# A four-layer transformer on one core: jobs of two layers take turns, a shorter prologue, and three areas for attention weights

## The chip, the cores and the metric

The kernel runs on one core of one Trainium2 chip. The metric is the device time of one launch in microseconds (us). Each core has a matrix engine (TensorE, in the rows PE, with its weight loads as PEld), a vector engine (VectorE, DVE), a scalar engine (ScalarE, ACT), GpSimd (POOL), and SyncE (SP), which here only issues transfers. Each engine works through its own list of instructions in order; they wait for each other by semaphores.

## The reference

Sixteen sequences of 256 tokens by 256 channels go through four different transformer layers, in float32. H is 16 heads of 16 channels; the context has 77 tokens of 256 channels.

```
x: (16, 256, 256)   context: (16, 77, 256)   cond: (16, 256)
L0: x += gate * self_attention(modulated_norm(x), rope, mask)
    x += gate * cross_attention(modulated_norm(x), context, key mask)
    x += gate * mlp(modulated_norm(x))           # gelu(tanh)
L1: x += cross_attention(modulated_norm(x), modulated_norm(context))
L2: x += gate * self_attention(...) ; x += cross_attention(...) ; x += gate * mlp(...)
L3: x += self_attention(..., rope)  ; x += cross_attention(..., rope) ; x += mlp(...)
modulated_norm(x) = norm(x) * (1 + scale) + shift
scale, shift, gate = (cond or silu(cond)) @ W + b    # ten pairs and five gates in all
```

## The kernel before, in words

**Jobs.** One sequence in one layer is a job; there are 64, numbered 0 to 63. Jobs 0 to 15 are L0, 16 to 31 L1, 32 to 47 L2, 48 to 63 L3. The text calls them "the first layer" to "the fourth layer" or L0 to L3. A job needs the stored result of the same sequence in the layer before. A job holds one of six slots (SLOTS), its number modulo six, from its start to its end, so that at most six jobs are under way; x, xhat, xnT and other tiles exist once per slot.

**Steps.** Each job is a list of steps, each one belonging to one engine. Self attention: the norm (ln, rs, nx), its transpose (xT, xe), projections (qkv), the split of queries and keys into a high and a low part (hi, lo), a round trip of these through memory that lays them out as stacked rows of q_stack and k_self or k_cross (ph, pw, lh, ll), scores by rows (S, `score_rows`) with row maxima on VectorE (mr, mx), the maxima placed by a transfer (sd), scores by columns (ST, `score_columns`), exponentials (ex), the weighted sums (W), transposes and division (oX, dv, atT), the output projection (out) and the residual (res). Cross attention is the same with 77 keys; the mlp has four steps up and two down.

**The plan.** `Program` writes out the order of each engine by playing the steps through a table of costs: each engine takes, of the steps whose buffers are free, the one with the lowest 12 * job - rank, rank being the cost of the chain behind it inside its job. Buffers are rings: four banks gen and two banks score of PSUM, three of max_tok and maxT (MAXIMA), three transposed contexts (CTX_T), four q_stack, and so on.

**Weights.** The attention blocks have two areas of SBUF, A and B, the mlp one, M. L0 self is in A, L0 cross in B, L1 in A, L2 self in B, L2 cross in A, L3 self in B, L3 cross in A. `load_weights` is a step of SyncE: it waits for the last user of the area in all 16 jobs and then issues the loads, so L2's cross weights wait for the last job of L1, L3's self weights for L2's last self block and L3's cross weights for L2's last cross block.

**Prologue.** A block of its own ahead of the main program. SyncE issues the constants, then all modulation matrices (7.8 MB with the rest), six small biases b_qk and the constant rows of k_self and k_cross. TensorE forms all ten modulations (line 698, 80 products) and five gates (706 and 707), VectorE adds the biases (668 to 679), the gates are stored to memory (607), and the main block starts. Its first instructions load the weights of L0 (1008) and the first x (934).

```
st = min(can, key=lambda st: (12 * st.job - st.rank
         - 4 * (eng == "pe" and TILES.get(st.name, "whole") == self.tiles), 0))
...
done = max(st.after, key=lambda res: res.nth_all)
sp.wait_ge(*moved(done.fill))
for dst, src in weight_dmas(st.blk):
    sp.dma_start(dst, src).then_inc(w_loaded[st.blk.area], 16)
```

## Time and profile before

| what | us |
|---|---|
| median of three runs | 2927.14 |
| lowest and highest run | 2912.56 and 2935.08 |
| the profiled execution, its own time | 2929.03 |
| its span, first to last instruction | 2927.2 |
| TensorE busy in the span | 2747.2 (94%) |
| VectorE, ScalarE, GpSimd busy | 1986.1, 1431.8, 288.1 |
| mean granted clock of TensorE | 0.963 |

The profile is of one execution. A granted clock of 1.00 is 2.4 GHz. Start times in the rows are counted from the first instruction. Matmuls overlap one another, so a busy time near the whole of a stretch does not say that the engine is at its peak; the busy time of the weight loads (PEld) is a second measure of the work done in it.

### The profile page before, as it was taken

What the parts mean: (1) busy time and instruction counts of PE and PEld (TensorE: products, weight loads), DVE (VectorE), ACT (ScalarE), POOL (GpSimd) and SP (SyncE); (2) the same over time, 40 slices, a digit from 0 to 9 for tenths busy, and PEclk for the clock granted to TensorE, in tenths of its full rate; (3) what the DMA queues carried; (4) which work ended last, traced back from release to release, by engine and by line L of the source; (5) the groups of instructions that cost most, each with busy time, mean ns of one, the idle gap of its engine ahead of it and who ended that gap; (6) DMA issues with size and microseconds to landing.
All of it is one profiled execution on the core that took longest, in us unless ns stands there. A gap on an engine that the chain in (4) does not pass through costs nothing.

```text
span 2927.2 us, 57672 instructions
## 1 busy us (share of the span) xinstructions
PE 2747.2 (94%) x21122; PEld 2021.6 (69%) x21122; DVE 1986.1 (68%) x5340; ACT 1431.8 (49%) x2281; POOL 288.1 (10%) x340
## 2 busy tenths in 40 slices
PE   6789999999999999989999999999989999999998
PEld 5456776776766766666677777776656777777666
DVE  2676776776765577777576777766677778777751
ACT  0335455455454445445455555554545554555553
POOL 0000000100101111101111111111000000000000
PEclk9999999999999999988899999999989999999999
DMA  4544334334333466644444444424245343433320
GB/s 130 154 151 138 110 115 133 104 118 130 104 96 113 125 193 183 186 145 127 147 136 138 127 143 121 149 82 151 77 135 170 90 141 106 134 113 120 121 73 15
DMA packets 279966, 369.40 MB, mean 126 GB/s; under 512 B 32506, under 2 KB 159034, under 8 KB 279372
## 3 DMA queue, kind: packets, MB, share of 16 engines
q1 hardware_dynamic: 247436, 318.63, 36.4%
q10 hardware_dynamic: 32256, 47.07, 4.4%
q8 instruction: 177, 2.90, 0.4%
q14 instruction: 97, 0.79, 0.1%
HBM read 224.49 MB, written 110.97 MB: 115 GB/s over the span
## 4 chain that ended last, share of the span: by engine, by line
PE 68%; DVE 17%; DMA 5%; issue 5%; ACT 1%; SPq 1%; POOL 0%; ACTq 0%; DVEq 0%; POOLq 0%
PE gen L1219 11%; PE gen L1228 10%; PE gen L1094 9%; PE gen L1060 9%; PE gen L1177 8%; DVE row_max L1516 6%; PE score L1152 4%; PE score L1107 3%; PE score L1122 3%; DMA parts_scratch<-parts 2%; PE gen L1188 2%; PE score L1136 2%; PE score L1158 2%; PE gen L1069 2%; DVE maxT L1535 2%
## 5 line engine op out<-in xcount | busy, mean ns | idle before, releaser
L1516 DVE TENSOR_REDUCE row_max<-score 128x4 f32<-128x1024 f32 (+1 forms) x640 | 651.8, 1044 | 131.1 <-PE score L1136 99.5
L1338 ACT ACTIVATE probs<-score 128x1024 f32<-128x1024 f32 (+1 forms) x576 | 567.3, 1023 | 289.5 <-PE score L1152 174.6
L1219 PE MATMUL gen<-xnT,w_w1M 128*128 128x256 f32 x1536 | 380.8, 397 | 1.9 <-ACT xnT L1283 1.8
L1228 PE MATMUL gen<-w_w2M,hT 128*128 128x256 f32 x1536 | 353.9, 384 | 8.1 <-DVE x L1567 4.7
L1370 POOL TENSOR_TENSOR rstd<-var_eps,minus_half 128x2 f32<-128x2 f32 x160 | 113.1, 707 | 2270.3 <-DVE var_eps L1413 2256.1
L1219 PEld LDWEIGHTS gen<-xnT,w_w1M 128*128 128x128 f32 x1536 | 290.1, 196 | 55.8 <-issue 2.8
L1228 PEld LDWEIGHTS gen<-w_w2M,hT 128*128 128x128 f32 x1536 | 286.1, 191 | 57.8 <-issue 18.9
L1283 ACT ACTIVATE xnT<-gen,mod_all 128x256 f32<-128x256 f32 x288 | 147.0, 565 | 211.2 <-PE gen L1069 205.7
L1360 ACT ACTIVATE hT<-gen,b_b 128x256 f32<-128x256 f32 x384 | 160.2, 472 | 170.4 <-PE gen L1219 169.5
L1345 ACT COPY oT<-gen 128x512 f32<-128x512 f32 x224 | 131.7, 588 | 182.8 <-PE gen L1177 180.2
L1535 DVE STREAM_TRANSPOSE maxT<-max_tok 32x64 f32<-32x64 f32 x896 | 209.0, 233 | 17.1
L1122 PE MATMUL score<-k_self,q_stack 64*128 64x256 f32 x1536 | 194.0, 342 | 25.3 <-DVE row_max L1516 23.8
L1177 PE MATMUL gen<-probs,v_self 128*17 128x256 f32 x3072 | 203.7, 386 | 0.0
L1565 DVE TENSOR_TENSOR xhat<-gen,gate 128x256 f32<-128x256 f32 (+1 forms) x112 | 60.2, 538 | 204.9 <-PE gen L1228 141.1
L1122 PEld LDWEIGHTS score<-k_self,q_stack 64*128 64x128 f32 x1536 | 128.5, 191 | 100.2 <-issue 81.4
L1152 PE MATMUL score<-q_stack,k_self 64*128 64x256 f32 x1536 | 187.3, 341 | 10.7 <-DMA q_stack<-maxT 5.4
L1152 PEld LDWEIGHTS score<-q_stack,k_self 64*128 64x128 f32 x1536 | 126.7, 194 | 75.3 <-issue 51.1
L1136 PEld LDWEIGHTS score<-k_cross,q_stack 64*128 64x128 f32 x2048 | 139.7, 195 | 49.4 <-issue 47.0
L1136 PE MATMUL score<-k_cross,q_stack 64*128 64x78 f32 x2048 | 158.5, 288 | 9.2 <-issue 3.9
L1177 PE MATMUL gen<-probs,v_cross 77*17 77x256 f32 x2048 | 159.9, 402 | 6.3 <-DVE parts L1477 2.8
L1188 PE MATMUL gen<-ident,oT 128*128 128x128 f32 x896 | 145.6, 288 | 0.1
L1544 DVE RECIPROCAL row_max<-gen 128x16 f32<-128x16 f32 x224 | 54.9, 245 | 128.4 <-PE gen L1188 127.8
(146 smaller groups left out, 4172.9 us busy)
## 6 DMA issues: line engine op xcount, KB each, us to landing
q_stack<-parts_scratch SPq DMA_DIRECT2D x336, 256.0 KB, 3.8
parts_scratch<-parts ACTq DMA_DIRECT2D x160, 256.0 KB, 2.8
parts_scratch<-parts SPq DMA_DIRECT2D x160, 256.0 KB, 3.3
k_self<-parts_scratch SPq DMA_DIRECT2D x144, 256.0 KB, 3.9
q_stack<-zeros_scratch SPq DMA_DIRECT2D x112, 256.0 KB, 3.9
q_stack<-maxT SPq DMA_DIRECT2D x224, 128.0 KB, 2.7
k_cross<-parts_scratch SPq DMA_DIRECT2D x192, 78.0 KB, 2.5
x_scratch<-x SPq DMA_DIRECT2D x48, 256.0 KB, 2.6
```

The source lines that it names most:

```text
L1060: mm = pe.matmul(out, xT[:, fc], weight[:, fc, cols], start=fc == 0, stop=fc == FC - 1)
L1094: mm = pe.matmul(out[:, c, :], weight[:, fc, cols], xT[:, fc, :], start=fc == 0, stop=fc == FC - 1)
L1122: mm = pe.matmul(buf[:, t, c * S:c * S + S], queries[rows, column(u), c * P:c * P + P], keys[rows, column(u), :], start=not blk.mask, stop ...
L1136: mm = pe.matmul(buf[:, t, at_col:at_col + CTXP], queries[rows, column(2 * u + i), c * P:c * P + P], keys[rows, column(2 * u + i), :], sta ...
L1152: mm = pe.matmul(buf[:, t, kc * S:kc * S + S], keys[rows, column(u), kc * P:kc * P + P], queries[rows, column(u), :], start=not blk.mask, ...
L1177: mm = pe.matmul(pv[VW * i:VW * i + VC, within, :], value, e, start=kc == 0, stop=not blk.whole or kc == TC - 1, skip_group_check=True)
L1188: mm = pe.transpose(buf[:, at_col:at_col + P], oT[before.buf][:, i, c * P:c * P + P], ident[:, :])
L1219: mm = pe.matmul(buf[:, i * S:i * S + S], w["M"]["w1"][:, fc, col:col + P], xnT[s][:, fc, :], start=fc == 0, stop=fc == FC - 1)
L1228: mm = pe.matmul(buf[:, 0:D], hT[:, j, c * P:c * P + P], w["M"]["w2"][:, j, :], start=j == 0, stop=j == FFC - 1)
L1338: act.activation(probs[st.probs][0:keys, :, :], score[st.fill.buf][0:keys, :, :].rearrange("p a (r q) -> p (a r) q", r=2), ACT.Exp, bias=k ...
L1516: dve.tensor_reduce(dst, src, AX_X, ALU.max).then_inc(max_done[b], 1)
L1535: ins = dve.transpose(maxT[st.got["max"]][:, :, 32 * b:32 * b + 32].bitcast(F32), max_tok[st.got["max"]][32 * b:32 * b + 32, :, :].bitcast ...
```

## The change

**Turns.** A table JOBS gives each job its layer and sequence. After L0 and the first eight jobs of L1, jobs of L2 and L1 alternate: L2 sequence 0, L1 sequence 8, L2 sequence 1, L1 sequence 9, ... up to L2 sequence 7, L1 sequence 15; then L2 sequences 8 to 15, then L3. Numbers of jobs, and with them slots and priorities, follow the table.

**Areas.** A third area C takes L1 and L3 self: its q and out parts lie in the two mask tiles (maskk and maskq, used by L0 self only) and its kv part is a new tile. L2 self is now in A, L2 cross in B, L3 cross in A. L1's biases have tiles of their own. To make room, MAXIMA and CTX_T go from three to two.

**Prologue.** Only L0's three modulations and gates are formed ahead of the main block. The other seven modulations (steps md on TensorE, ma on VectorE) and two gates (mg, mh, and the store ms) are steps of the plan; their matrices are loaded into tiles that are not yet in use (w1, w2, kv of B, hT), five in the prologue and two (la) in the main program. L0's self weights and the first two x are loaded in the prologue. The weights of L0's cross and mlp wait for the sums that read those tiles. The small biases are issued by GpSimd.

```diff
-MAXIMA = 3
+MAXIMA = 2
-CTX_T = 3
+CTX_T = 2
...
-    [Block("L1", "cross", "A", 1e-5, mod=3, qk_bias=0, out_bias=True, ctx="norm", ctx_mod=4)],
-    [Block("L2", "self", "B", 1e-6, mod=5, qk_bias=2, out_bias=True, gate=3),
-     Block("L2", "cross", "A", 1e-6, qk_bias=4, out_bias=True, ctx="norm"),
+    [Block("L1", "cross", "C", 1e-5, mod=3, qk_bias=0, out_bias=True, ctx="norm", ctx_mod=4, behind=(0, 0))],
+    [Block("L2", "self", "A", 1e-6, mod=5, qk_bias=2, out_bias=True, gate=3),
+     Block("L2", "cross", "B", 1e-6, qk_bias=4, out_bias=True, ctx="norm"),
...
-    [Block("L3", "self", "B", 1e-5, mod=7, rope=S),
+    [Block("L3", "self", "C", 1e-5, mod=7, rope=S),
...
+GATES_EARLY = 3
+LATE = [Late("adaln2", 0, 3 * D, "w1", "M", 5, D, 0, True, gate=3),
+        Late("adaln2", 3 * D, 3 * D, "w2", "M", 6, D, 0, True, gate=4),
+        Late("adaln3a", 0, 2 * D, "kvB", "B", 7, 0, D, False),
+        Late("adaln1q", 0, 2 * D, "hT0", "hid", 3, 0, D, True),
+        Late("adaln1kv", 0, 2 * D, "hT1", "hid", 4, 0, D, True),
+        Late("adaln3b", 0, 2 * D, "hT0", "hid", 8, 0, D, False, then=3),
+        Late("adaln3c", 0, 2 * D, "hT1", "hid", 9, 0, D, False, then=4)]
+LEAD = 8
+JOBS = [(0, seq) for seq in range(B)] + [(1, seq) for seq in range(LEAD)]
+for turn in range(B - LEAD):
+    JOBS += [(2, turn), (1, LEAD + turn)]
+JOBS += [(2, seq) for seq in range(B - LEAD, B)] + [(3, seq) for seq in range(B)]
...
+        w["C"] = {"q": maskk[:, :, :].bitcast(F32), "kv": sb("w_kvC", shapes["kv"]), "out": maskq[:, :, :].bitcast(F32)}
...
-                    for dst, src in const_loads:
+                    for dst, src in const_loads[:4]:
                         sp.dma_start(dst, src).then_inc(const_loaded, 16)
-                    for key, name in ada_loads:
-                        sp.dma_start(ada[key][:, :, :], a[name].rearrange("(c p) n -> p c n", p=P)).then_inc(adaln_loaded[key], 16)
...
+                    sp.dma_start(ada[:, :, :], a["adaln0"].rearrange("(c p) n -> p c n", p=P)).then_inc(adaln_loaded, 16)
...
+                    for st in plan.order["sp"]:
+                        if st.early and st.name == "ldw":
+                            for dst, src in weight_dmas(st.blk):
+                                sp.dma_start(dst, src).then_inc(w_loaded[st.blk.area], 16)
...
+                    for i, late in enumerate(LATE):
+                        if late.then is None:
+                            dst, src = late_dma(i)
+                            sp.dma_start(dst, src).then_inc(late_loaded[i], 16)
...
+                def modulation_sums(st):
+
+                    late = LATE[st.j]
+                    pe.wait_ge(late_loaded[st.j], 16)
+                    buf, c = fill(st), siluT if late.silu else condT
+                    for kind, first in enumerate((late.scale, late.shift)):
+                        for fc in range(FC):
+                            col, n = first + fc * P, kind * FC + fc
+                            for kc in range(FC):
+                                mm = pe.matmul(buf[:, n * B:n * B + B], wide[late.tile][:, kc, col:col + P], c[:, kc, :], start=kc == 0, stop=kc == FC - 1)
+                    mm.then_inc(gen_full[st.buf], 1)
```

The diff changes the order of the instructions in three places of which the prediction speaks. TensorE's list at the start of the main program, before, from the second branch on: transposes of the first x (xhat), projections from area A, the context's from area B, then the first scores with their mask product.

```order
L1034 UNCONDITIONAL_BRANCH
L1069 MATMUL gen<-ident,xhat 128x128 x8
L1094 MATMUL gen<-xnT,w_qA 128x256 x8
L1094 MATMUL gen<-xnT,w_kvA 128x256 x8
L1060 MATMUL gen<-w_kvA,xnT 128x256 x8
L1080 MATMUL gen<-ident,ctx_in 128x77 x4
L1094 MATMUL gen<-ctxT,w_kvB 128x77 x8
L1060 MATMUL gen<-w_kvB,ctxT 77x256 x4
L1107 MATMUL score<-maskq,pick 128x512 x4
L1122 MATMUL score<-k_self,q_stack 128x256 x4
```

The same place now, in two pieces:

```order
L1124 UNCONDITIONAL_BRANCH
L1330 MATMUL gen<-condT,w_kvB 128x16 x8
L1159 MATMUL gen<-ident,xhat 128x128 x4
L1330 MATMUL gen<-siluT,w_w1M 128x16 x8
L1184 MATMUL gen<-xnT,w_qA 128x256 x4
```

```order
L1150 MATMUL gen<-w_kvB,ctxT 77x256 x2
L1330 MATMUL gen<-siluT,w_w2M 128x16 x8
L1197 MATMUL score<-maskq,pick 128x512 x4
L1212 MATMUL score<-k_self,q_stack 128x256 x4
L1197 MATMUL score<-maskq,pick 128x512 x4
L1212 MATMUL score<-k_self,q_stack 128x256 x4
L1330 MATMUL gen<-siluT,hT 128x16 x8
L1197 MATMUL score<-maskq,pick 128x512 x4
L1212 MATMUL score<-k_self,q_stack 128x256 x4
L1197 MATMUL score<-maskq,pick 128x512 x4
L1212 MATMUL score<-k_self,q_stack 128x256 x4
L1330 MATMUL gen<-siluT,hT 128x16 x8
```

Late sums (line 1330) now stand first, between the first transpose and its projection, ahead of the first scores, and between pairs of them; two late gates follow among the scores and two more sums among the first ST.

SyncE's list around the load of L2's cross weights (in_L_cq, in_L_ckv, in_L_co), before:

```order
L968 DMA q_stack<-zeros_scratch 32x4x512
L978 DMA q_stack<-parts_scratch 32x4x512 x2
L988 DMA q_stack<-parts_scratch 32x4x512
L1008 DMA w_qA<-in_L_cq 128x2x256
L1008 DMA w_kvA<-in_L_ckv 128x2x512
L1008 DMA w_outA<-in_L_co 128x2x256
L1008 DMA b_ckv<-in_L_bkv 128x256
L1008 DMA b_co<-in_L_bo 128x256
L968 DMA q_stack<-zeros_scratch 32x4x512
L1001 DMA x_scratch<-x 128x2x256
```

and now:

```order
L1056 DMA k_cross<-parts_scratch 32x4x156
L1036 DMA q_stack<-zeros_scratch 32x4x512
L1081 DMA w_qB<-in_L_cq 128x2x256
L1081 DMA w_kvB<-in_L_ckv 128x2x512
L1081 DMA w_outB<-in_L_co 128x2x256
L1081 DMA b_ckv<-in_L_bkv 128x256
L1081 DMA b_co<-in_L_bo 128x256
L1024 DMA parts_scratch<-parts 128x512
L1000 DMA x_in<-x_scratch 128x2x256
```

Before, the load stood beside the store of L1's last job, at place 655 of 1281 rows; now it stands at place 441, beside L1's third job, where L0's last cross block ends.

TensorE's list in the middle of L1, before, where all steps are L1's (weights in A):

```order
L1094 MATMUL gen<-ctxT,w_kvA 128x77 x4
L1060 MATMUL gen<-w_kvA,ctxT 77x256 x2
L1199 MATMUL gen<-ident,xhat 128x128 x4
L1136 MATMUL score<-k_cross,q_stack 128x78 x8
L1158 MATMUL score<-q_stack,k_cross 77x256 x4
L1069 MATMUL gen<-ident,xhat 128x128 x4
L1060 MATMUL gen<-w_outA,xnT 128x256 x4
L1158 MATMUL score<-q_stack,k_cross 77x256 x8
L1177 MATMUL gen<-probs,v_cross 17x256 x4
L1094 MATMUL gen<-xnT,w_qA 128x256 x4
```

and now, in the stretch of turns (self scores with k_self and w1 of L2, w_kvB from L2 cross, w_kvC, maskq and maskk from L1):

```order
L1150 MATMUL gen<-w_kvB,ctxT 77x256 x2
L1184 MATMUL gen<-ctxT,w_kvC 128x77 x4
L1150 MATMUL gen<-maskq,xnT 128x256 x4
L1212 MATMUL score<-k_self,q_stack 128x256 x8
L1159 MATMUL gen<-ident,xhat 128x128 x4
L1212 MATMUL score<-k_self,q_stack 128x256 x4
L1309 MATMUL gen<-xnT,w_w1M 128x256 x4
L1212 MATMUL score<-k_self,q_stack 128x256 x4
L1242 MATMUL score<-q_stack,k_self 128x256 x4
L1309 MATMUL gen<-xnT,w_w1M 128x256 x12
```

Steps of an L1 job stand between those of three L2 jobs at different stages.

## Rows read from the trace of the kernel before

**Rows 1.** The page, parts 1 and 2: busy times, and 40 slices of TensorE.

```profile
PE 2747.2 (94%) x21122; PEld 2021.6 (69%) x21122; DVE 1986.1 (68%) x5340; ACT 1431.8 (49%) x2281; POOL 288.1 (10%) x340
...
PEclk9999999999999999988899999999989999999999
```

**Rows 2.** Busy time by stretch; columns as in the first line.

```profile
core 0: us, PE busy (x) PEld busy (x) DVE busy (x) ACT busy (x) POOL busy (x), PEclk, DMA share, GB/s
75.00:250.00 175.00, 145.83 (x1232) 99.91 (x1234) 118.82 (x276) 65.30 (x99) 5.12 (x8) 0.93 0.47 147
300.00:850.00 550.00, 538.34 (x4442) 394.19 (x4439) 378.69 (x954) 273.93 (x420) 42.86 (x52) 1.00 0.38 117
1060.00:1204.00 144.00, 134.94 (x1136) 96.80 (x1132) 107.60 (x373) 73.17 (x133) 23.40 (x28) 0.91 0.61 183
1204.00:1460.00 256.00, 231.88 (x1774) 161.21 (x1774) 173.23 (x477) 119.01 (x192) 28.81 (x34) 0.88 0.49 148
1600.00:1875.00 275.00, 275.00 (x2149) 205.99 (x2149) 204.18 (x556) 151.36 (x246) 46.87 (x53) 1.00 0.44 133
1950.00:2250.00 300.00, 273.39 (x2000) 201.01 (x1999) 211.57 (x550) 151.05 (x236) 26.25 (x29) 0.93 0.41 128
2300.00:2750.00 450.00, 433.09 (x3353) 322.89 (x3351) 353.00 (x908) 242.48 (x382) 30.22 (x36) 0.99 0.39 121
```

**Rows 3.** Timeline, SyncE: loads of weights after L1 and L2, stores of finished jobs.

```profile
1060.93 0.38 SPq L1001 DMA_DIRECT2D x_scratch<-x  x1
...
1204.93 0.38 SPq L1001 DMA_DIRECT2D x_scratch<-x  x1
...
1374.32 0.39 SPq L1008 DMA_DIRECT2D w_qA<-in_L_cq  x1
...
1636.08 0.38 SPq L1001 DMA_DIRECT2D x_scratch<-x  x1
...
1873.02 0.38 SPq L1001 DMA_DIRECT2D x_scratch<-x  x1
...
1996.01 0.39 SPq L1008 DMA_DIRECT2D w_qB<-in_L_qkv  x1
...
2145.36 0.39 SPq L1008 DMA_DIRECT2D w_qA<-in_L_cq  x1
```

**Rows 4.** Timeline, the prologue and the first steps of the main program.

```profile
14.06 10.39 PE L698 MATMUL gen<-condT,ada 128*128 128x16 f32 x48 [3.90 <-DMA ada<-in_adaln]
...
44.77 3.57 PE L698 MATMUL gen<-condT,ada3c 128*128 128x16 f32 x16
...
48.27 1.89 PE L706 MATMUL score<-ada,condT 128*16 128x256 f32 x4
...
51.05 1.89 PE L706 MATMUL score<-ada,condT 128*16 128x256 f32 x4
...
61.21 1.03 PE L707 MATMUL score<-gate_bias,ones 1*16 1x256 f32 x2
...
65.26 0.40 SPq L1008 DMA_DIRECT2D w_qA<-in_L_qkv  x1
...
71.12 0.75 DVE L1407 BATCH_NORM_STATS2 stats<-x_in 128x6 f32<-128x256 f32 x2 [8.43 <-DMA x_in<-in_x]
...
75.20 1.09 PE L1069 MATMUL gen<-ident,xhat 128*128 128x128 f32 x4 [12.95 <-DVE xhat L1419]
```

**Rows 5.** Timeline of TensorE at the first scores.

```profile
105.40 1.03 PE L1107 MATMUL score<-maskq,pick 64*128 64x512 bf16 x4 [10.89 <-DMA k_self<-parts_scratch]
...
111.84 0.61 PE L1107 MATMUL score<-maskq,pick 64*128 64x512 bf16 x4 [0.29 <-DVE row_max L1516]
...
112.97 0.61 PE L1107 MATMUL score<-maskq,pick 64*128 64x512 bf16 x4 [0.29 <-DVE row_max L1516]
113.21 0.60 PE L1122 MATMUL score<-k_self,q_stack 64*128 64x256 f32 x4
115.45 0.61 PE L1107 MATMUL score<-maskq,pick 64*128 64x512 bf16 x4 [1.64 <-DVE row_max L1516]
```

**Rows 6.** The page, parts 5 and 6: ScalarE's move of xT; the maxima's transfer, us to landing.

```profile
L1283 ACT ACTIVATE xnT<-gen,mod_all 128x256 f32<-128x256 f32 x288 | 147.0, 565 | 211.2 <-PE gen L1069 205.7
...
q_stack<-maxT SPq DMA_DIRECT2D x224, 128.0 KB, 2.7
```

**Rows 7.** Stores of jobs (L1001): first and last start of the group.

```profile
L1001 SPq DMA_DIRECT2D x_scratch<-x x48: 360/377/594, 285.9 to 2205.8; - x48
```

**Rows 8.** Weight loads of one projection, in 1060 to 1204 and on the page.

```profile
L1060 PEld LDWEIGHTS gen<-w_outA,xnT 128*128 128x128 f32 x72 | 15.7, 227 | 2.7
...
L1228 PEld LDWEIGHTS gen<-w_w2M,hT 128*128 128x128 f32 x1536 | 286.1, 191 | 57.8 <-issue 18.9
```

More of the change, by code:

```diff
@@ L134, in __init__ @@
         self.buf = self.n = None
+        self.early = False
         self.prior, self.got, self.times = {}, {}, {}
@@ L204, in __init__ @@
         self.step, self.steps, self.ends, self.weights = {}, [], {}, {}
-        for job in range(len(LAYERS) * B):
+        self.gates_late = []
+        self.late_modulations()
+        for job in range(len(JOBS)):
             self.job_steps(job)
@@ L234, in job_steps @@
         kept = self.ends.get((job - SLOTS, "stx"))
-        last = early = self.add(job, 0, first, "ldx", 0, "sp", [self.ends.get((job - B, "stx"))])
+        last = early = self.add(job, 0, first, "ldx", 0, "sp", [self.ends.get((PLACE.get((li - 1, seq)), "stx"))])
+        if job < X_IN:
+            self.load_early(last)
         gate_free = left
@@ L1279, in modulated @@
                 def modulated(st, out, buf, pair, width, stride):
+                    if pair >= GATES_EARLY and not late_known:
+                        late_known.append(True)
+                        act.wait_ge(mod_added, len(LATE))
                     for fc in range(FC):
```

339 lines of the change are left out of this document (213 added, 126 removed).

## The prediction

> **What bounds the kernel now.** I read the busy times first. TensorE is busy 2747.2 of 2927.2 us, the next engine 1986.1, so TensorE's list sets the time, and its gaps, with the slices in which its granted clock is under 9 tenths or so, are where something can be won [rows 1]. Then the stretches. From 1600 to 1875 us, the steady part of L2, TensorE is busy in all of 275.0 us at a granted clock of 1.00, and its weight loads fill 205.99, a share of 0.749 [rows 2]. No change of order can win anything there. Four stretches are looser: the start (75 to 250, clock 0.93), L1 (1060 to 1204, clock 0.91), the passage into L2 (1204 to 1460, clock 0.88) and that into L3 (1950 to 2250, clock 0.93) [rows 2]. VectorE has 107.6 of 144 us in L1, ScalarE less, so neither is the bound there either; what is missing is TensorE's time, in short gaps and in slower matmuls.
>
> I measure the looseness by weight loads, at the share of a nearby dense stretch. Start: 99.91 over L0's 394.19/550 = 0.717 is 139 us of work in 175, so 36 lost. L1: 96.80/0.749 = 129 in 144, 15 lost over nine jobs. Into L2: 161.21/0.749 = 215 in 256, 41 lost. Into L3: 201.01 over the fourth layer's 322.89/450 = 0.718 is 280, or 268 at 0.749, in 300: 20 to 32 lost, 26 in the middle [rows 2].
>
> The Trainium skill (Perfetto Trace Analysis, Identifying the Most-Contended Engine) says that matmul busy time misleads about the room left, and that the busy share of the weight loads is the thing to use. The trace agrees in so far as busy PE reads 134.94 of 144 in L1, 9 us of room, where the loads give 15 [rows 2]. By matmul gaps alone the passage into L2 would hold 24 us and the one into L3 27, and the forecast below would be some 20 us later.
>
> The reason for the loss after 1204 is in SyncE's timeline. L2's cross weights are issued at 1374.32, when the last L1 job has ended; until then six slots fill with L2 jobs that can only do their self part. L3's self weights are issued at 1996.01 and its cross weights at 2145.36, the same pattern [rows 3].
>
> **The prologue.** Removed from it: seven modulations and two gates. Ahead of the main block now stand one wait for L0's matrix, 10.39 us of products (48 records, start 14.06) and three gates at 51.05 - 48.27 = 2.78 us, 8.3. That ends at 32.8. From the last gate product's end (61.21 + 1.03 = 62.24) to the main block's first instruction (65.26) are 3.0 us: 35.8. The first x is there already, so the 5.9 us from 65.26 to the statistics at 71.12 go too, and these start at about 35.9 instead of 71.12: 35.2 us earlier [rows 4].
>
> The removed sums come back in the main program: seven at 3.57 us and two gates at 1.89 us, 28.8 us of TensorE [rows 4]. Three of them stand before the first scores. The first runs while x is normalised (4.1 us from 71.12 to 75.20) and costs nothing; the second delays the first projection by up to 3.6, less the 1.1 us of ScalarE's two instructions at 565 ns [rows 6], 2.5; the third falls in the wait of 10.89 us for k_self [rows 4, 5]. Two sums and two gates stand between the eight score steps. These go at VectorE's pace, 1.13 to 2.2 us each where TensorE needs 0.9, so some 3 of the 10.9 us are hidden and 8 are not [rows 5]. The last two, 7.1 us, stand among the first ST steps; I take 5 as open. Together 16, rounded to 15 because a busier TensorE is granted its clock sooner. Start: -35.2 + 15 = **-20**. Bounds: everything hidden, -35; nothing hidden, -6. If the first sum's matrix lands late, behind L0's and the first weights, the whole start waits for it; the first 14 us moved data for the matrix that TensorE waited 3.90 us for [rows 4]. That is inside the upper bound.
>
> L0's cross and mlp weights now wait for sums. The cross weights for the first sum, which is first in the list; the mlp's for the two gates, long before the mlp that ends job 0 at 285.9 [rows 7]. Covered. What queues behind these waits on SyncE are the stores and placements of jobs 0 and 1, which the third term above has already delayed. The small biases go from SyncE to the idle GpSimd, and their first user is in L1.
>
> **The turns.** Before, a steady L2 job takes (1873.02 - 1636.08)/5 = 47.4 us and an L1 job (1204.93 - 1060.93)/9 = 16.0 [rows 3]; by its weight loads an L1 job is 129/9 = 14.4 us of dense work. Eight L1 jobs now stand between L2 jobs, and L2's cross weights come in before L1 has got far. If a pair runs as densely as steady L2 it takes 14.4 + 47.4 = 61.8 us, and the change wins the 41 us of the passage and 8 * 1.6 = 13 us in L1, 54 together. VectorE has room in a pair: 107.60/9 + 204.18/(275/47.4) = 12.0 + 35.2 = 47 of 61.8 [rows 2]. What speaks against the whole 54 are the slots. In steady L2 six jobs share them, so that one may last 6 * 47.4 = 284 us. In turns only three are L2's, and one may last 3 * 61.8 = 185 us, or TensorE waits. Steps of one job therefore stand closer together in the list, and some will wait for a transfer or an exponential. I take 1.75 us for each pair, 14: **-40**. Bounds: 0, if a pair keeps L1's looseness and the passage's; and 85, since the same kind of load takes 227 ns in L1 where another takes 191, so that loads overstate the work of the loose stretches by a tenth or more [rows 8] (145/0.749 = 194 of 256, 62 lost, and 23 in L1).
>
> **Into L3.** Its self weights wait only for L1, and its cross weights for L2's self blocks, whose last ends near 1996, where before they came at 2145.36 [rows 3]. The mlp weights wait as before for the last L2 mlp. I take two thirds of 26: **-17**, bounds 0 and -32.
>
> **The rings.** With two max_tok, a third `negate_maximum` waits until the first one's transfer has landed, 2.7 us [rows 6]. What stands behind it on VectorE are row maxima, for which TensorE waits. Two per job come in a row and the next job's a few us later, so few meet; **+3**, bounds 0 and +15 (one in forty of 224 paying in full is 15).
>
> **Sum.** Against the profiled execution's own 2929.0: -20.2 - 40 - 17 + 3 = -74.2, 2854.8. The median of the runs is 1.9 under that execution, so I predict **2853 us**, with 2830 to 2885 as this case's own range.
>
> **Rivals.**
> - Nothing is lost in the turns: the pairs are dense and the late sums mostly hidden. -30 at the start, -54, -26: 2817 us. For it speaks that L0 and L2 hold a clock of 1.00 over hundreds of us [rows 2]; against it the 185 us.
> - The slots bind. Job 0 lasted from 75.20 to 285.9, 210.7 us, though partly cold and with masks [rows 4, 7]. If an L2 job in turns needs that, a pair takes 210.7/3 = 70.2 us, 8 * 8.4 = 67 us more than dense: the turns cost 13 instead of winning 40, and the time is 2906.
> - Slower than before: the same mechanism, further on. It turns the sign of the whole when a pair loses more than (54 + 34)/8 = 11 us, where an L2 job lasts 219 us. At 240 us a pair takes 80, the turns cost 92 and the time is 2985. Against it: with half of the jobs in flight being short ones, an L2 job waits less for others than job 0's successors did.
> - The start does nothing because the first late sum waits for its matrix: some 14 us later than forecast, 2867, inside my own range.
>
> The Trainium skill (Perfetto Trace Analysis, Optimization Strategy) advises to interleave stretches whose most contended engine differs. Here TensorE leads in both [rows 2], so by that rule alone the turns would win little, and what I count on is the missing wait for weights.
>
> **How the numbers follow.** Chances: the forecast 0.64, nothing lost 0.17, slots bind 0.13, slower 0.06. A measurement of this kernel tells about 1% (29 us) from no change. Faster by over 1% (under 2898) take the first two and a little of the third, 0.83; within 1% most of the third, 0.12; slower 0.05. The range goes from inside the second case to the third's time, 2808 to 2908.
>
> **What would show it.** Right: the first transpose of x near 40 us instead of 75.20; L2's cross weights issued before 1050 us; stores of L2 jobs about 62 to 64 us apart in turns, with a granted clock near 1.00 and weight loads at 0.72 or more there; no stretch at 0.88; the stretch into L3 at a load share near 0.70. Wrong: pairs of 70 us, gaps of several us before ST or down steps of the same job, a first projection after 50 us, or VectorE rows that wait at the maxima's transfer.

## The result, and the profile after

| | before | after |
|---|---|---|
| median of the runs, us | 2926.61 (4 runs, 2912.56 to 2935.08) | 2877.11 (4 runs, 2876.59 to 2889.28) |
| ratio, 95% interval | | 0.9838, 0.981 to 0.9865 |
| span of the profiled execution, us | 2927.2 | 2875.3 |
| mean granted clock | 0.963 | 0.969 |

The change makes the kernel faster by 1.6% by the ratio; by the medians it is 49.5 us, where 74 were forecast. With four runs on each side, differences of two kernels below are sure to some 5 to 10 us, and the ratios give other differences than the medians: where it matters both are named. The page of the changed kernel first, the rows that answer to [rows 1].

```profile
PE 2718.9 (95%) x21118; PEld 2005.6 (70%) x21118; DVE 1995.6 (69%) x5348; ACT 1444.6 (50%) x2293; POOL 291.6 (10%) x346
...
PEclk9999999999999998999999998999999999999999
```

Before, slices 18 to 20 and 30 had an 8 in PEclk; now slices 16 and 25 have one, the latter from 1725 to 1797 us, where there was dense L2 before. Next the view of [rows 2], with the turns and the way out of them cut where they lie now.

```profile
core 0: us, PE busy (x) PEld busy (x) DVE busy (x) ACT busy (x) POOL busy (x), PEclk, DMA share, GB/s
75.00:250.00 175.00, 156.59 (x1329) 106.82 (x1328) 125.97 (x308) 74.97 (x110) 8.21 (x11) 0.95 0.41 133
1215.00:1480.00 265.00, 251.91 (x2005) 187.58 (x1998) 192.16 (x556) 147.95 (x242) 41.96 (x48) 0.97 0.45 140
1540.00:1820.00 280.00, 262.31 (x2014) 189.23 (x2006) 192.28 (x546) 142.71 (x227) 36.74 (x43) 0.90 0.44 139
1820.00:1895.00 75.00, 74.80 (x568) 56.64 (x568) 59.27 (x146) 39.51 (x68) 14.14 (x16) 1.00 0.43 128
1950.00:2250.00 300.00, 292.41 (x2271) 216.69 (x2270) 233.60 (x600) 163.62 (x257) 24.00 (x28) 1.00 0.42 132
```

The turns (1215 to 1480) run at a load share of 187.58/265 = 0.708 and a clock of 0.97, better than the old passage into L2 (0.88) and worse than steady L2 (0.749 and 1.00). Then comes a stretch that did not exist before: from 1540 to 1820, the way out of the turns, the share is 0.676 and the clock 0.90. Before, the same 280 us lay mostly in dense L2. After it, one dense stretch, and the way into L3 now runs at 0.722 and a clock of 1.00, against 0.670 and 0.93.

SyncE's timeline answers to [rows 3].

```profile
976.42 0.59 SPq L1081 DMA_DIRECT2D w_qB<-in_L_cq  x1
...
1206.70 0.37 SPq L1069 DMA_DIRECT2D x_scratch<-x  x1
...
1540.07 0.38 SPq L1069 DMA_DIRECT2D x_scratch<-x  x1
...
1613.02 0.38 SPq L1069 DMA_DIRECT2D x_scratch<-x  x1
...
1707.37 0.38 SPq L1069 DMA_DIRECT2D x_scratch<-x  x1
...
1768.93 0.47 SPq L1081 DMA_DIRECT2D maskk<-in_L_qkv  x1
...
1803.57 0.59 SPq L1069 DMA_DIRECT2D x_scratch<-x  x1
...
1985.58 0.39 SPq L1081 DMA_DIRECT2D w_qA<-in_L_cq  x1
```

L2's cross weights come 398 us earlier, L3's self weights 227 and its cross weights 160 earlier. From 1206.70 to 1540.07 five pairs pass, 66.7 us each; forecast were 63.5. The two stores of L2 jobs behind 1613.02 each come 94 and 96 us after the one before, with one L2 and one L1 job between, and a dense pair was put at 62.

TensorE's timeline at the start answers to [rows 4, 5].

```profile
37.96 3.57 PE L1330 MATMUL gen<-condT,w_kvB 128*128 128x16 f32 x16 [2.87 <-PEq L712]
41.37 1.09 PE L1159 MATMUL gen<-ident,xhat 128*128 128x128 f32 x4
...
45.53 3.76 PE L1184 MATMUL gen<-xnT,w_qA 128*128 128x256 f32 x8
...
64.96 0.61 PE L1197 MATMUL score<-maskq,pick 64*128 64x512 bf16 x4 [1.06 <-DMA k_self<-parts_scratch]
```

The first transpose of x stands at 41.37 where 40 was forecast and 75.20 was before; the first scores wait 1.06 us where they waited 10.89. The first projection stands at 45.53, under the 50 us that the prediction named as a sign of being wrong.

**A second reading.** For the comparisons below I follow TensorE's steps in each trace, count every step at a usual duration of its kind in the trace of before, and note when the same sum is reached. The difference of the two times is what has been gained up to there. For the changed kernel it is 27 us after the start, 20 at 1173 us (in L1), 69 at 1435, 39 at 1715, 21 at 1855, 54 at 2240, and 52 at the end. So up to 1435, where the turns are in full course, 42 us were won behind the start, and 48 were lost on the way out of them. The two ends of this, 20 at 1173 and 21 at 1855, are the firm part: nearly the same work lies behind both kernels there. In the middle they have done different mixtures of L1 and L2, and the reading depends on the durations taken. Counted by the median distance from one product's start to the next in the trace of before, it is 22 at 1173, 80 at 1435, 43 at 1715 and 20 at 1855.

### The profile page after: what moved, and what is told of

It reads as the page before. It is cut to its first block, busy times and chain, and to the rows that moved or that the text cites. A ratio compares the mean times of both kernels' runs of the same rounds, so it can differ in the third digit from the quotient of the medians.

```text
span 2875.3 us, 57738 instructions
## 1 busy us (share of the span) xinstructions
PE 2718.9 (95%) x21118; PEld 2005.6 (70%) x21118; DVE 1995.6 (69%) x5348; ACT 1444.6 (50%) x2293; POOL 291.6 (10%) x346
## 4 chain that ended last, share of the span: by engine, by line
PE 68%; DVE 18%; issue 6%; DMA 4%; ACT 1%; SPq 1%; POOL 0%; ACTq 0%; DVEq 0%; POOLq 0%
PE gen L1309 12%; PE gen L1318 11%; PE gen L1184 9%; PE gen L1150 8%; PE gen L1267 8%; DVE row_max L1641 6%; PE score L1242 4%; PE score L1197 3%; PE score L1212 3%; PE score L1248 2%; PE gen L1278 2%; DMA parts_scratch<-parts 2%; PE gen L1159 2%; PE score L1226 2%; DVE maxT L1660 2%
## 5 line engine op out<-in xcount | busy, mean ns | idle before, releaser
L1309 PE MATMUL gen<-xnT,w_w1M 128*128 128x256 f32 x1536 | 383.0, 399 | 3.1 <-ACT xnT L1400 3.1
L1309 PEld LDWEIGHTS gen<-xnT,w_w1M 128*128 128x128 f32 x1536 | 291.8, 197 | 57.9 <-ACT xnT L1400 5.0
L1212 PE MATMUL score<-k_self,q_stack 64*128 64x256 f32 x1536 | 192.3, 341 | 26.7 <-DVE row_max L1641 25.5
L1212 PEld LDWEIGHTS score<-k_self,q_stack 64*128 64x128 f32 x1536 | 127.8, 191 | 96.1 <-issue 77.0
```

The costliest lines, as they stand in the source:

```text
L1212: mm = pe.matmul(buf[:, t, c * S:c * S + S], queries[rows, column(u), c * P:c * P + P], keys[rows, column(u), :], start=not blk.mask, stop ...
L1309: mm = pe.matmul(buf[:, i * S:i * S + S], w["M"]["w1"][:, fc, col:col + P], xnT[s][:, fc, :], start=fc == 0, stop=fc == FC - 1)
```

## The experiments

Ratios are to the kernel before. All twelve diffs are to the changed kernel, but for the one that says otherwise.

**No turns.** The jobs are in the old order, all else stays.

```diff
-LEAD = 8
+LEAD = 16
```

> The changed kernel with LEAD = 16: all of L1 runs before L2, no turns, everything else (areas, prologue, rings of two) stays. Theory A (the turns win at their start and lose the same where they end, because the slots of short L1 jobs refill with L2 jobs that are too close together): without turns the slots refill in the same way at the end of L1, only once, so the time stays at 2870 to 2885 us. Theory B (the turns themselves are too slow, 66.9 us for a pair against 61.8, since three slots are too few for L2): without them the missing wait for L2's cross weights is won in full and the time is 2840 to 2855. If the turns are what wins, it is over 2900.

Measured: 2867.99 us, 0.9788 (0.9772 to 0.9804). That interval lies wholly below the changed kernel's (0.981 to 0.9865): the turns cost 9 us by the medians and 15 by the ratios, and no theory that gave them a gain stands. It is also below what Theory A expected, 2870 to 2885. Its stretches:

```profile
1150.00:1400.00 250.00, 223.51 (x1712) 155.25 (x1711) 178.43 (x505) 114.36 (x192) 27.09 (x33) 0.88 0.53 163
1400.00:1860.00 460.00, 459.54 (x3619) 343.78 (x3618) 333.69 (x923) 257.88 (x418) 78.24 (x89) 1.00 0.44 132
1950.00:2250.00 300.00, 292.72 (x2263) 216.79 (x2261) 231.91 (x603) 162.21 (x256) 23.62 (x28) 0.99 0.44 136
```

The passage into L2 is as loose as before the change (load share 0.621 beside 0.630 [rows 2], clock 0.88 in both), though the weights for L2's cross attention are there at 978.97 us. Then 460 us without a gap. The way into L3 is as good as in the changed kernel.

**The prologue alone.** No turns, and the areas of the kernel before.

```diff
-LEAD = 8
+LEAD = 16
...
-    [Block("L1", "cross", "C", 1e-5, mod=3, qk_bias=0, out_bias=True, ctx="norm", ctx_mod=4, behind=(0, 0))],
-    [Block("L2", "self", "A", 1e-6, mod=5, qk_bias=2, out_bias=True, gate=3),
-     Block("L2", "cross", "B", 1e-6, qk_bias=4, out_bias=True, ctx="norm"),
+    [Block("L1", "cross", "A", 1e-5, mod=3, qk_bias=0, out_bias=True, ctx="norm", ctx_mod=4)],
+    [Block("L2", "self", "B", 1e-6, mod=5, qk_bias=2, out_bias=True, gate=3),
+     Block("L2", "cross", "A", 1e-6, qk_bias=4, out_bias=True, ctx="norm"),
...
-    [Block("L3", "self", "C", 1e-5, mod=7, rope=S),
+    [Block("L3", "self", "B", 1e-5, mod=7, rope=S),
```

> The changed kernel with LEAD = 16 and the areas as before (L1 in A, L2 self in B, L2 cross in A, L3 self in B): what is left of the change is the prologue and the rings of two. From the two traces the start is worth 27 us and stays so to the end: 2899 us, with the weight loads of L2's cross block at about 1347 again. If the rings of two cost something elsewhere, 2902 to 2912.

Measured: 2903.02 us, 0.9915 (0.989 to 0.9939). The prologue gives 23.5 us by the medians; the areas 2903.0 - 2868.0 = 35 us on top.

**The rings alone.** The kernel before, with two instead of three buffers.

```diff
-MAXIMA = 3
+MAXIMA = 2
-CTX_T = 3
+CTX_T = 2
```

> The kernel before with MAXIMA = 2 and CTX_T = 2 and nothing else. Forecast of the prediction: +3 us, at most +15. Theory C (the rings take back part of the change): +8 to +15. Theories A and B: 0 to +3.

Measured: 2926.03 us, 1.0002 (0.9988 to 1.0017), ten runs. The rings cost nothing.

**Two L2 jobs for each L1 job.**

```diff
-LEAD = 8
+LEAD = 10
...
-    JOBS += [(2, turn), (1, LEAD + turn)]
-JOBS += [(2, seq) for seq in range(B - LEAD, B)] + [(3, seq) for seq in range(B)]
+    JOBS += [(2, 2 * turn), (2, 2 * turn + 1), (1, LEAD + turn)]
+JOBS += [(2, seq) for seq in range(2 * (B - LEAD), B)] + [(3, seq) for seq in range(B)]
```

> The changed kernel with ten L1 jobs first and then two L2 jobs for each of the last six of L1, so that the turns reach nearly to the end of L2 and four slots of six are L2's. Theory A: the passage out of the turns is softer (one slot in three instead of one in two changes over) and lies near the passage into L3, so 2850 to 2862 us. Theory B: a group of two L2 and one L1 takes about 110 us instead of 114, with a job allowed 218 us, 2855 to 2865, and the stretch behind the turns keeps its loss. If neither (the order of jobs does not matter), 2877.

Measured: 2958.02 us, 1.0076 (1.004 to 1.0112), slower than before: every expectation was far off. The stretches of one group and its repetition say how:

```profile
1385.00:1454.00 69.00, 68.43 (x511) 52.12 (x510) 47.71 (x133) 35.29 (x60) 15.78 (x17) 1.00 0.34 106
1511.00:1580.00 69.00, 68.43 (x511) 52.14 (x510) 48.42 (x135) 35.30 (x60) 15.79 (x17) 1.00 0.35 105
1454.00:1511.00 57.00, 53.12 (x358) 35.93 (x357) 34.80 (x98) 26.04 (x41) 2.63 (x4) 0.76 0.44 143
```

A group takes 126 us: 69 at full clock without a gap, then 57 with 4 us of gaps and a clock of 0.76. In those 57 us TensorE waits for the row maxima of scores several times (gaps of 0.2 to 1.4 us at L1212 and L1248). The trace shows a second difference: the 69 us hold eight mlp steps of the kind up (L1309), the 57 us none. What that does is told below, with the turns.

**Mirrored turns.** L2, L1, L1, L2, so that each slot holds L2 and L1 jobs in turn.

```diff
-for turn in range(B - LEAD):
-    JOBS += [(2, turn), (1, LEAD + turn)]
+for turn in range(0, B - LEAD, 2):
+    JOBS += [(2, turn), (1, LEAD + turn), (1, LEAD + turn + 1), (2, turn + 1)]
```

> The changed kernel with the order inside every second pair mirrored: L2, L1, L1, L2 instead of L2, L1, L2, L1. In the changed kernel the even slots hold L2 jobs alone and the odd ones L1 jobs alone: L2 jobs last 193 to 199 us there, a third of that is 66, and the pairs take 66.9. Mirrored, every slot holds an L2 and an L1 job in turn, so that both together may last six pairs, 370 us at 61.8. Theory A, the slots bind the turns (the rival of the prediction): the pairs come down to 62 or 63 us, eight times 4 us, 2845 and in any case under 2860. Theory B, the pairs are loose for another reason (the mixture of steps, the passages in and out of the turns): pairs of 66 to 68 us and 2870 to 2885.

Measured: 2894.46 us, 0.9876 (0.9851 to 0.9902). Two pairs, between stores at 1462.78 and 1597.32, take 67.3 us each. Theory A falls: with the slots shared out the pair does not come down to 62. Theory B named the pairs rightly; the time lies above its 2870 to 2885. The number of slots, six, was not changed, so that this run speaks against the division of the slots and not against their number.

**Four turns.**

```diff
-LEAD = 8
+LEAD = 12
```

> The changed kernel with turns for the last four L1 jobs instead of the last eight. Theory A, each pair costs (66.9 less 61.8, 5 us): four pairs less win 20 us, 2857. Theory B, the passage out of the turns costs, where 47 us were lost between 1440 and 1815, and is there once however many pairs stand before it: 2877, within 6. Theory C, the loss at the way out grows with the number of L1 jobs that still hold slots, which is four here as there: also 2877. Without turns at all it was 2868, so a value between 2863 and 2872 would say that the turns and their passages only balance each other.

Measured: 2890.72 us, 0.9865 (0.9843 to 0.9887), above every expectation, clearly above no turns, and 14 us above eight turns by the medians (those intervals overlap a little). So the cost neither grows with the pairs nor is it one fixed sum at the exit. The gain read at the same work is 24 us at 888, 7 at 1186, 30 at 1382, 10 at 1578, and 6 until L3's start: 17 us are lost where L2 comes in, 23 are won, and 20 are lost again where L1 ends.

**L1 first, with turns.** 60 off the priority number of L1's steps.

```diff
-                st = min(can, key=lambda st: (12 * st.job - st.rank - 4 * (eng == "pe" and TILES.get(st.name, "whole") == self.tiles), 0))
+                st = min(can, key=lambda st: (12 * st.job - st.rank - 60 * (st.li == 1) - 4 * (eng == "pe" and TILES.get(st.name, "whole") == self.tiles), 0))
```

> The changed kernel, with 60 taken from the priority number of every L1 step (12 for each job's number, less the rank), so that the list prefers it. In the turns L1's steps lose against those of later L2 jobs whose rank is higher: L1's last job held its slot from 1531.6 to 1767.8, 236 us, where its first held one for about 95. Theory A, these held slots are what makes the passage out of the turns loose: L1 jobs of 100 to 130 us, and half of the 47 us lost at the way out come back, 2855. Theory B, what counts there is that the L2 jobs come in the same phase, self scores after self scores: no gain, 2872 to 2890, as the L2 jobs are then held up by L1 steps.

Measured: 2949.39 us, 1.0067 (1.0041 to 1.0092), 72 us worse than the change, outside both expectations. L2's stores in the turns:

```profile
1269.75 0.38 SPq L1069 DMA_DIRECT2D x_scratch<-x  x1
...
1350.70 0.38 SPq L1069 DMA_DIRECT2D x_scratch<-x  x1
...
1423.11 0.38 SPq L1069 DMA_DIRECT2D x_scratch<-x  x1
...
1502.10 0.38 SPq L1069 DMA_DIRECT2D x_scratch<-x  x1
```

77.5 us per pair. By TensorE's first and last step of each job, L1 jobs last mostly 80 to 96 us and L2 jobs 211 to 227 instead of 193 to 199, and each L2 job starts 5 to 6 us after the last one of its slot has ended: 227 + 5 over three slots is the pair. Here the slots do bind. The L2 jobs, pushed back by L1's steps, are longer, and L1's three slots stand empty for most of the time: one from 1204 to 1330 us, and the last five L1 jobs each start 104 to 142 us after the end of the job before it in its slot, where in the changed kernel that is 13 to 16.

**Half of the late sums left out.** Only the first half of the contraction of the seven late modulations is computed, so that the result differs from the reference. In the diff, the operands are cut (...).

```diff
-                            for kc in range(FC):
-                                mm = pe.matmul(..., start=kc == 0, stop=kc == FC - 1)
+                            for kc in range(1):
+                                mm = pe.matmul(..., start=True, stop=True)
```

> The changed kernel with half of each of the seven late modulations left out (only the first 128 of the 256 channels of the condition are summed), four matmul groups of one instead of two. It takes 12.5 us of TensorE's 25.0 out of the late sums. Theory A, as the prediction has it, about half of the sums' time is exposed: 6.5 us less, 2870.5. Theory B, they are wholly hidden: 2877, within 2. Theory C, wholly exposed, since the start is bound by TensorE's list: 2864.5.

Measured: 2878.52 us (five runs, 2868.95 to 2885.55), 0.9829 (0.9804 to 0.9855). The whole time cannot tell. The trace says more: at the same work this kernel has gained 31.9 us behind the start, where seven kernels with whole sums and the same order up there have 23.2 to 29.2, mean 26.1. So about 6 us came back; it is one trace against seven, and they scatter by 6. But these are not 6 of 12.5, as the expectation had it. By TensorE's timeline the seven sums and two gates together take 18.9 us in the changed kernel and 20 to 23 in the other kernels with whole sums, and 13.3 us here: 6 to 9 us were taken out. Most of them came back, more than the half of Theory A, as far as one trace can say.

**L3's weights wait as before.**

```diff
-     Block("L3", "self", "C", 1e-5, mod=7, rope=S),
-     Block("L3", "cross", "A", 1e-5, mod=8, rope=S, ctx="raw"),
+     Block("L3", "self", "C", 1e-5, mod=7, rope=S, behind=(2, 0)),
+     Block("L3", "cross", "A", 1e-5, mod=8, rope=S, ctx="raw", behind=(2, 1)),
```

> The changed kernel with L3's loads waiting as before: its self weights for L2's last self block, its cross weights for L2's last cross block; the areas stay as changed. The prediction put 17 us on the way into L3, bounds 0 and 32; compared at the same amount of TensorE's work, the changed kernel gained 36 us between 1950 and 2250 us. Theory A, all of that is the missing wait for weights: 2877 + 36 = 2913, and the cross weights come at about 2100 us. Theory B, as forecast: 2894. Theory C, part of the gain is that L2's last jobs are spread otherwise after the turns: between the two, and above 2900 only if the turns have no share in it.

Measured: 2906.02 us (2899.41 to 2924.53), 0.9914 (0.9888 to 0.994), 29 us over the changed kernel. Its stretch and its loads:

```profile
1950.00:2250.00 300.00, 274.09 (x1992) 201.77 (x1991) 211.03 (x547) 151.03 (x233) 26.22 (x29) 0.93 0.40 129
```

```profile
1990.32 0.39 SPq L1081 DMA_DIRECT2D maskk<-in_L_qkv  x1
...
2138.04 0.39 SPq L1081 DMA_DIRECT2D w_qA<-in_L_cq  x1
```

Load share 0.673 and clock 0.93, the values of before [rows 2]: into L3 the missing wait is the cause. Its price is 29 us by the medians and 22 by the ratios, between Theories A and B; the rest of the 36 is within the scatter of single traces (this one's own execution, 2924.53 us, lies 18.5 over its median).

**L2's cross weights wait as before, no turns.**

```diff
-LEAD = 8
+LEAD = 16
...
-     Block("L2", "cross", "B", 1e-6, qk_bias=4, out_bias=True, ctx="norm"),
+     Block("L2", "cross", "B", 1e-6, qk_bias=4, out_bias=True, ctx="norm", behind=(1, 0)),
```

> The changed kernel without turns (2868), and with L2's cross weights waiting for the last job of L1 as before. The prediction held that the wait for these weights is why the passage into L2 is loose. Theory A, it is: 2868 + 30 to 40 = 2900 or more. Theory B, the passage is loose because six L2 jobs start within 200 us and come through the same phase, with or without weights: 2868 to 2880. For B speaks that without turns, and with the weights there at about 975 us, only 8 us were gained between 1150 and 1460.

Measured: 2869.2 us (2862.76 to 2877.72), 0.9798 (0.9769 to 0.9827), beside 2868.0 and 0.9788 (0.9772 to 0.9804) without the wait.

```profile
1353.79 0.39 SPq L1081 DMA_DIRECT2D w_qB<-in_L_cq  x1
```

The weights come 375 us later, and the time is the same within some 10 us. Theory B: the 30 to 40 us of Theory A are ruled out. A small cost is not: from 1150 to 1400 us the clock is 0.85 here and 0.88 without the wait, at nearly the same loads (156.71 and 155.25 us).

**The row maxima over half of the keys.** In L2's self attention VectorE takes the maximum over 128 of 256 keys; another number is subtracted ahead of the exponential, in numerator and denominator alike.

```diff
+                        src = src[:, :, :, 0:S // 2] if st.li == 2 else src
```

> The changed kernel, where the row maxima of L2's self attention are taken over the first 128 of the 256 keys: VectorE's instruction there gets shorter, from about 1.1 us to some 0.6, and what is computed changes by rounding alone. In the changed kernel 7.5 of TensorE's idle us between 1540 and 1820 are ended by these row maxima, and after such a stretch the granted clock is low for some 40 us. Theory A, VectorE's row maxima are what makes the turns and the way out of them loose, and the clock multiplies it: 25 to 40 us less, 2840 to 2852. Theory B, the idle time alone is won and the clock stays: 8 to 12 us, 2867. Theory C, it is the order and mixture of steps: within 5 of 2877.

Measured: 2851.46 us (2848.19 to 2857.38), 0.9738 (0.9717 to 0.9759), 26 us under the changed kernel by the medians, 29 by the ratios: Theory A, at the edge of its span. The group of row maxima (1215 to 1540) and TensorE's waits (1540 to 1820), first of the changed kernel:

```profile
L1641 DVE TENSOR_REDUCE row_max<-score 128x4 f32<-128x1024 f32 x40 | 47.0, 1219 | 1.4 <-PE score L1212 1.4
```

```profile
PE score L1212 <- DVE row_max L1641: 7.5, 11, 2.2
```

and of this one, with its stretch on the way out:

```profile
L1642 DVE TENSOR_REDUCE row_max<-score 128x4 f32<-128x512 f32 x40 | 26.2, 686 | 2.0 <-PE score L1212 1.4
```

```profile
PE score L1212 <- DVE row_max L1642: 3.1, 6, 1.1
```

```profile
1540.00:1820.00 280.00, 268.47 (x2058) 197.23 (x2059) 180.49 (x566) 146.05 (x237) 39.00 (x46) 0.93 0.46 144
```

The waits for these maxima fell by 4.4 us, the loads done in the same 280 us rose by 8.0, and the clock from 0.90 to 0.93. Read at the same work, it gains on the changed kernel 7 us up to 1435, 12 up to 1572, 17 up to 1715, 23 up to 1855, and nothing more behind it. Behind 1855 L2 is dense, with TensorE busy for 74.80 of the 75 us from 1820 on in the changed kernel; so this is the price of the maxima in the turns and at their exit.

**L1 first, no turns.**

```diff
-LEAD = 8
+LEAD = 16
...
-                st = min(can, key=lambda st: (12 * st.job - st.rank - 4 * (eng == "pe" and TILES.get(st.name, "whole") == self.tiles), 0))
+                st = min(can, key=lambda st: (12 * st.job - st.rank - 40 * (st.li == 1) - 4 * (eng == "pe" and TILES.get(st.name, "whole") == self.tiles), 0))
```

> The changed kernel without turns (2868), and with 40 taken from the priority number of L1's steps. Without turns L1's last three jobs held their slots for 119, 148 and 168 us beside the first L2 jobs, where steady ones take 55 to 90. Theory A, the held slots delay the L2 jobs and with them the dense part: 2855 to 2862. Theory B, as with the turns (L1 first cost 72 us there): the L2 jobs are held up by as much, 2868 to 2880.

Measured: 2851.10 us (2838.81 to 2865.85), 0.9736 (0.9697 to 0.9775): level with the halved maxima, 2.6% under before and 26 us under the changed kernel. Against no turns it is 17 us by the medians, and the intervals still touch.

```profile
1150.00:1400.00 250.00, 229.30 (x1840) 162.18 (x1839) 188.27 (x535) 123.77 (x207) 33.85 (x39) 0.93 0.54 171
```

In the passage into L2 6.9 us more of loads and a clock of 0.93 instead of 0.88. Read at the same work it is 3 us behind no turns at 1182 and 13 ahead at 1274, and keeps that. Theory A in direction, 4 us under its span. With turns the same kind of edit, with 60 for 40, cost 72 us.

## Why the prediction came out near, and where its steps failed

The terms against what the runs give them, by medians:

| term | forecast | measured |
|---|---|---|
| start | -20 | -23.5 |
| rings | +3 | 0 (in the start's) |
| turns and the passage into L2 | -40 | +9, and -6 of the areas (late L2 weights account for 1 of it, the rest no run attributes) |
| into L3 | -17 | -29 |
| sum | -74 | -49.5 |

**The time came near by luck.** The largest term failed: turns and passage were to win 40 us and cost 3, 9 lost by the turns and 6 won by the areas. With +3 in place of -40 the same sum gives 2896 us, outside the stated 2830 to 2885. The other three terms were all too cautious, by 3.5, 3 and 12 us, and that brought the sum back to -49.5. Of the named signs, the early transpose, the early weights and the stretch into L3 came; pairs of 62 to 64 us did not, the load share in the turns was 0.708 for 0.72, and a loose stretch (0.90) appeared where dense L2 had been.

**Start: near, with one price wrong.** The first transpose came at 41.37 us, 33.8 earlier. 27 us of that are left behind the start by the changed kernel's trace, 26 as the mean of seven. So 7 or 8 us are exposed late sums, where the working put 15. The price of one sum was too high: 3.57 us, read from the prologue, gave 28.8 us for all sums and gates, and the changed kernel's timeline has 18.9. Only the first two sums take 3.57 and 3.43 us; from 62 us on a sum takes 1.85 to 2.22, with weight loads of about 192 ns each where they took 333. (In most of the variants the fourth and fifth take 3.59 too, and the whole is 20 to 23 us.) The granted clock does not show this in the rows of the start: the trace's clock records begin at 49.7 us, at 81.0 in the kernel before, and ahead of them the view prints 1.00. The wait of 10.89 us for k_self has become 1.06, filled by a sum and by work of the second job.

**Rings: too high.** The forecast put three us on something that the ten runs put at 0, within 5.

**Into L3: right mechanism, sized too small.** The forecast took two thirds of 26 us lost. The wait alone gives 29 by the medians, 22 by the ratios. The 26 came from load shares, with a bound of 32 by the other divisor, and both are inside; so the third that I held back for L2's mlp weights was largely not lost. The share there is 0.722 now, forecast near 0.70.

**Turns: wrong, and this is the step that failed.** "The reason for the loss after 1204 is in SyncE's timeline" was the sentence. It read two facts side by side, slots filled with L2 jobs that cannot go on and a loose TensorE, and made one the cause of the other. With the wait and without it the kernel takes 2869.2 and 2868.0 us. What the loose places have in common is another thing: the eight self score steps of an L2 job go through without mlp steps of another job between them, and there TensorE goes at VectorE's pace. This is such a place at the exit from the turns in the changed kernel, with the last mlp step up (L1309) ahead of it and the first behind it:

```profile
1601.54 1.89 PE L1309 MATMUL gen<-xnT,w_w1M 128*128 128x256 f32 x8
...
1636.31 0.74 PE L1212 MATMUL score<-k_self,q_stack 64*128 64x256 f32 x8
1639.27 0.50 PE L1212 MATMUL score<-k_self,q_stack 64*128 64x256 f32 x4 [2.22 <-DVE row_max L1641]
1640.40 0.80 PE L1212 MATMUL score<-k_self,q_stack 64*128 64x256 f32 x4 [0.63 <-DVE row_max L1641]
1641.53 0.79 PE L1212 MATMUL score<-k_self,q_stack 64*128 64x256 f32 x4 [0.33 <-DVE row_max L1641]
...
1644.93 0.71 PE L1248 MATMUL score<-q_stack,k_cross 64*77 64x256 f32 x4 [0.33 <-DVE row_max L1641]
...
1677.37 1.99 PE L1309 MATMUL gen<-xnT,w_w1M 128*128 128x256 f32 x8
```

Score steps stand one behind the other with nothing between; TensorE needs 0.5 to 0.8 us for one and starts one each 1.13 us, as VectorE's maxima allow. From 1600 to 1660 us line 1212 has 32 products, eight steps of four: all of this is one job. And this is dense L2, in the kernel without turns:

```profile
1533.49 0.50 PE L1212 MATMUL score<-k_self,q_stack 64*128 64x256 f32 x4
1533.92 1.99 PE L1309 MATMUL gen<-xnT,w_w1M 128*128 128x256 f32 x8
1535.85 0.50 PE L1212 MATMUL score<-k_self,q_stack 64*128 64x256 f32 x4
1536.28 1.99 PE L1309 MATMUL gen<-xnT,w_w1M 128*128 128x256 f32 x8
```

The other traces bear this out. Line 1212's steps, taken by the program's order, make 16 self score phases of L2 in each trace. I counted, in the trace of before and in those of the changed kernel and eleven variants, the phases without a step up in them, and the time at which the clock's records stand at the lower level (1.2 GHz) within such a phase or in the 25 us behind it. The table has the kernels that load L3's weights early, in order of time:

| kernel | phases without up | low clock there, us | median us |
|---|---|---|---|
| L1 first, no turns | 4 | 31 | 2851.1 |
| halved maxima | 4 | 34 | 2851.5 |
| no turns | 4 | 51 | 2868.0 |
| no turns, L2's weights wait | 5 | 58 | 2869.2 |
| changed kernel | 4 | 61 | 2877.1 |
| half of the late sums | 4 | 58 | 2878.5 |
| four turns | 5 | 81 | 2890.7 |
| mirrored turns | 6 | 82 | 2894.5 |
| L1 first, with turns | 11 | 174 | 2949.4 |
| two for one | 9 | 182 | 2958.0 |

Of 70 phases without a step up, 67 have low clock in or behind them, 14 us in the mean; of 110 with three or four, 6 have. Half of the time at the lower level is lost, by the two levels: between no turns and two for one that is (182 - 51)/2 = 66 of 90 us. In no trace do the self scores of two L2 jobs overlap, so jobs that come through one phase together, which the expectations of several runs speak of, are not what is seen. In the passage into L2 without turns the first step up stands at 1392.6 us: the first L2 jobs come through self attention before any of them has reached its mlp. Behind the turns every other job ahead was an L1 job, which has no mlp: steps up come in groups at 1591, 1677 and 1782 us, 86 to 105 us apart, and self score phases at 1579, 1631, 1673, 1727 and 1776. The phases at 1631 and 1727 have none, and behind these two the clock falls. That the missing mlp steps are the cause is read from the traces; no run changed them alone.

The forecast checked VectorE over a pair, 47 of 61.8 us, which was right as a mean (192.16/265 = 0.73 busy) and said nothing of a stretch of ten us.

So by the second reading the turns did win where they began, 42 us up to 1435 (forecast 40 with the loss of the pairs), but not for the reason given, and what they won was lost again where they end, 48 us. The size of both depends on how the work is counted; that they cancel does not. The forecast had no term for the way out. What it had as a doubt, 1.75 us for each pair, measured 5 (66.7 less 61.8).

**The rival "slots bind" was half right.** Pairs of 66.7 us lie between the forecast's 63.5 and its 70.2, L2 jobs follow each other in a slot within 4 to 7 us, and L1 first shows that a longer L2 job makes a longer pair. But mirrored turns, where no slot is L2's alone, stay at 67.3: in the changed kernel the slots are full, and their division is not the reason. Whether six slots are too few for pairs of 62 us no run tests.

The Trainium skill (Perfetto Trace Analysis, Optimization Strategy) says that interleaving can pay where the most contended engine changes from one stretch to the next. In the prediction this stood for a low gain of the turns; the runs agree in so far as they gained nothing (2877.1 us with, 2868.0 without). Its next sentences, to find the gaps of the leading engine and what blocks each of them, are the step that was left out: TensorE's waits in the passage into L2 (1204 to 1460), in the kernel before, had said it:

```profile
PE score L1122 <- DVE row_max L1516: 6.3, 10, 1.8
PE gen L1069 <- DVE xhat L1419: 4.5, 2, 2.5
```

The row maxima stand first (9.4 of some 23 us with all their rows), and no wait for weights is among them.

**What stays open.** That the maxima of L2's self attention cost 26 us in this order is shown, by halving them. That it is the phases without mlp steps, and not the amount of VectorE's work, rests on the traces: no run put such steps in or took them out alone, and none halved the maxima without turns. Four turns have more of these phases than eight or none, which fits their time and does not prove the reason. How the 35 us of the areas divide is known for 29 of them (22 by the ratios), and these were measured with turns.

## To carry to other kernels

A loose stretch with a late load in it is not yet loose because of the load: put the wait back, or take it away, by itself, and look at the time. Where a job has a run of steps that another engine paces, ask which steps of other jobs stand between them, and look at the places where a pipeline fills, changes its mixture of jobs or drains: an order that supplies them at one place may starve them at another, and here the whole gain was given back. And where the granted clock falls behind short gaps, as in these traces, count a gap at the bottleneck for more than its length.

## What the hardware showed that was not expected

Short gaps are followed here by stretches at a lower clock that cost more than the gaps. The way out of the turns in the changed kernel, in six pieces:

```profile
1600.00:1640.00 40.00, 36.83 (x292) 28.67 (x291) 26.29 (x77) 17.08 (x31) 3.80 (x5) 1.00 0.44 139
1640.00:1680.00 40.00, 37.77 (x284) 24.41 (x285) 24.18 (x66) 23.39 (x33) 5.38 (x6) 0.74 0.37 120
1680.00:1700.00 20.00, 20.00 (x132) 15.97 (x131) 16.84 (x45) 13.90 (x24) 3.06 (x4) 1.00 0.47 152
1700.00:1740.00 40.00, 35.48 (x280) 26.70 (x278) 29.70 (x75) 11.30 (x21) 4.68 (x6) 0.91 0.43 134
1740.00:1780.00 40.00, 39.67 (x316) 26.26 (x317) 22.14 (x76) 24.62 (x36) 5.39 (x6) 0.75 0.42 132
1780.00:1820.00 40.00, 39.68 (x286) 29.68 (x284) 30.60 (x85) 21.31 (x35) 5.87 (x7) 1.00 0.51 159
```

The first 40 us have 3.2 us without a matmul at a clock of 1.00, and the next 40 run at 0.74; the same again from 1700, with 4.5 us open and then 0.75. The clock's records have the lower level, 1.2 GHz, from 1640.3 for 20.5 us and from 1735.9 for 23.9 us, each time from the middle of a phase of bare score steps on. That costs some 10 us of full speed each time, behind 3 to 5 us of gaps. The longest single gap in the first of these pieces is the 2.22 us of the bunch shown above. In the second case TensorE was busy for 39.67 of the 40 us at the low clock, so that nothing in its busy time shows it.

The other surprise is the scatter of single traces: seven kernels whose TensorE has the same order of steps up to 300 us stand 6 us apart there. Differences under that can't be read from one profile.
